# The queries' normed rows are turned by VectorE and placed by DMA instead of being turned by TensorE, and the order of products is rewritten

## The chip, the core and the metric

The kernel runs on one core of one Trainium2 chip, all in fp32. Its metric is the device time of one execution in microseconds (us). Engines are named as in the profile: PE is TensorE's matmul, PEld its weight load, DVE VectorE, ACT ScalarE, POOL GpSimd, SP SyncE. SP and POOL issue nearly all DMAs. Each engine runs its own program in order; a semaphore wait holds everything behind it on that engine.

## The reference

```python
x = x + xattn(layernorm(x), ctx, ctx, Wq, Wk, Wv, Wo)   # 8 batches of 512 rows of 256, ctx 1601 rows
x = x + ffn(layernorm(x), ...)                          # shared FFN and 16 experts, top 64 rows each

def xattn(query, key, value, Wq, Wk, Wv, Wo):           # 16 heads of 16
    q = (query @ Wq.T) * scale; k = key @ Wk.T; v = value @ Wv.T
    scores = sigmoid(q k^T)                             # per head, no softmax
    return (scores @ v) @ Wo.T
```

## The kernel before

**Stages.** The attention of batches b = 0 to 7 runs first; the FFN follows. In each batch's attention there are 52 "quads": 4 quarters of 13 tiles of 128 context rows. A quad is two pairs, each of them S (2 matmuls, L1751, scores of two heads into one of three PSUM banks `score0..2`) and an ACT sigmoid (L876) from the bank to SBUF, and then one W (8 matmul records, L1780, probabilities times values, into `acc` or `misc`).

**Products.** Beside batch b's quads PE makes what batch b + 1 needs: K (keys, L1566), V (values, L1580), Q (queries, L1589), T (the normed rows of x turned, so that rows stand along the free axis, L1597), and what is left of batch b - 1: O (output projection, L1607) and G (gate logits, L1649, into `misc`). All but G go into the same ring of three score banks: whatever stands three ring entries later (S or product) may start only when the entry before it in that bank has been read, by ACT for an S, by DVE for a product (`wait_slot`).

**Order.** The strings OPENING (batch 0), EACH (1 to 6) and CLOSING (7) give PE's order: a letter S or W, or T for "the next product" of the list that `beside(b)` returns. ACT and DVE take up the work in that order. DVE has further work that is keyed to quads (`beside_quad(b, q)`, called at the odd S of quad q): for the residual rows of batch b - 1 the sums at q 9, the scale at 11, `norm_apply` and `turn_norm` (32x32 block transposes into `norm_blocks`) at 12 and `split_norm` at 22; for the x rows of batch b + 1 sums at 15, scale at 17, apply at 19 (17, 19, 21 in batch 0).

**Placing.** DVE's transposes turn 32x32 blocks only. `place_norm` on POOL moves the blocks with 16 DMAs of 32 KB (L765); it waits until SP's two stores of the batch (`norm_scr`, `resid_scr`, semaphore `post_stored`) have landed. `split_norm` waits for all 16 (`norm_placed`) and makes a high and a low part (`nt_hi`, `nt_lo`), which SP stores at q 24. After that store (`nt_stored`) the T products of x fill the same two tiles, `turned_rows` reading them from PSUM, and Q reads them.

**Tiles.** `xn` holds x and then its normed rows; `resid` holds x again (loaded by SP at q 24) to take the O products of the next batch.

## Time and profile before

| what | us |
|---|---|
| median of 3 runs | 1311.09 (1307.8 to 1319.05) |
| the profiled run, its time | 1305.85 |
| the profiled execution, its span | 1304.0 |
| the attention part, to the start of the FFN | about 892 |
| one batch, 1 to 6 | 109.0 |
| PE busy / ACT busy in such a batch | 108.3 / 98.8 |

The clock that TensorE was granted is 1.00 of full speed in every window. PE is busy in all but 0.7 us of a batch by the profile's count, ACT nine tenths of it, DVE 54%, POOL a tenth. A busy PE is not a PE without waits, since the records of matmuls in flight overlap; the starts of its instructions tell more than its busy share.

### The profile page before, as it was taken

What the parts mean: (1) busy time and instruction counts of PE and PEld (TensorE: products, weight loads), DVE (VectorE), ACT (ScalarE), POOL (GpSimd) and SP (SyncE); (2) the same over time, 40 slices, a digit from 0 to 9 for tenths busy, and PEclk for the clock granted to TensorE, in tenths of its full rate; (3) what the DMA queues carried; (4) which work ended last, traced back from release to release, by engine and by line L of the source; (5) the groups of instructions that cost most, each with busy time, mean ns of one, the idle gap of its engine ahead of it and who ended that gap; (6) DMA issues with size and microseconds to landing.
All of it is one profiled execution on the core that took longest, in us unless ns stands there. A gap on an engine that the chain in (4) does not pass through costs nothing.

```text
span 1304.0 us, 25503 instructions
## 1 busy us (share of the span) xinstructions
PE 1283.8 (98%) x10200; PEld 772.1 (59%) x10200; DVE 732.5 (56%) x1377; ACT 985.3 (76%) x1148; POOL 286.9 (22%) x288
## 2 busy tenths in 40 slices
PE   8999999999999999999999999999999999999997
PEld 6445444444454544544444443336888888888887
DVE  6564475365266448437536633215558777777773
ACT  5888989998998899899999989996333455555553
POOL 3000030020002003002000200500001567677635
PEclk9999999999999999999999999999999999999999
DMA  7785973874776597387477549713543577777754
GB/s 215 179 188 126 139 184 111 125 162 133 130 139 166 118 137 171 113 131 148 149 129 140 127 93 156 169 34 114 195 130 110 181 201 192 188 192 190 192 109 49
DMA packets 118726, 190.82 MB, mean 146 GB/s; under 512 B 22448, under 2 KB 71600, under 8 KB 118608
## 3 DMA queue, kind: packets, MB, share of 16 engines
q1 hardware_dynamic: 98768, 155.21, 51.9%
q0 software_dynamic: 19648, 33.72, 12.4%
q8 instruction: 81, 1.33, 0.5%
q10 hardware_dynamic: 192, 0.26, 0.1%
q14 instruction: 37, 0.30, 0.1%
HBM read 108.43 MB, written 55.61 MB: 126 GB/s over the span
## 4 chain that ended last, share of the span: by engine, by line
PE 87%; issue 5%; DMA 2%; DVE 2%; ACT 2%; POOL 1%; SPq 0%; POOLq 0%; DVEq 0%; ACTq 0%
PE score L1839 19%; PE score L1751 18%; PE acc L1780 14%; PE misc L1780 13%; PE score L1857 9%; PE score L1566 5%; PE score L1580 5%; PE score L1589 2%; ACT probs L876 1%; PE score L1619 1%; PE score L1607 1%; DMA key_scr<-key_parts 1%; POOL norm L765 1%; DMA norm<-norm_blocks 1%; DMA ctx_raw<-ctx_t 1%
## 5 line engine op out<-in xcount | busy, mean ns | idle before, releaser
L876 ACT ACTIVATE probs<-score 128x1024 f32<-128x1024 f32 (+1 forms) x832 | 789.8, 1026 | 77.3 <-PE score L1751 70.6
L1751 PE MATMUL score<-queries,keys 48*128 48x512 f32 (+1 forms) x1664 | 312.2, 438 | 6.5 <-ACT probs L876 4.2
L1751 PEld LDWEIGHTS score<-queries,keys 48*128 48x128 f32 (+1 forms) x1664 | 139.1, 180 | 275.0 <-ACT probs L876 212.7
L1780 PE MATMUL acc<-probs,values 128*32 128x512 f32 (+1 forms) x1664 | 210.5, 601 | 0.0
L1780 PE MATMUL misc<-probs,values 128*32 128x512 f32 (+1 forms) x1664 | 205.8, 600 | 0.0
L1026 DVE TENSOR_REDUCE whole<-score 128x512 f32<-128x1024 f32 (+1 forms) x75 | 77.0, 1026 | 196.6 <-PE score L1566 119.6
L729 POOL DMA_DIRECT2D ctx_raw<-ctx_t x32 | 23.4, 733 | 642.6 <-DVE ctx_lo L1004 557.9
L801 POOL DMA_INDIRECT gathered<-norm_scr,gather_row x64 | 81.2, 1269 | 227.5 <-DVE gather_row L1374 212.2
L891 ACT ACTIVATE gelu<-score 128x512 f32<-128x512 f32 (+1 forms) x97 | 55.5, 580 | 84.6 <-PE score L1839 84.0
L814 POOL DMA_INDIRECT out<-result,add_row x64 | 106.6, 1666 | 48.4 <-ACT result L944 25.9
L1839 PE MATMUL score<-tok_hi,gu_hi 128*128 128x512 f32 (+1 forms) x388 | 117.0, 383 | 0.0
L1839 PE MATMUL score<-tok_lo,gu_hi 128*128 128x512 f32 (+1 forms) x388 | 116.2, 381 | 0.0
L1839 PE MATMUL score<-tok_hi,gu_lo 128*128 128x512 f32 (+1 forms) x388 | 116.2, 381 | 0.0
L1321 DVE TENSOR_TENSOR hidden<-gelu,score 128x512 f32<-128x512 f32 (+1 forms) x97 | 64.0, 664 | 92.6 <-PE score L1839 62.3
L899 ACT ACTIVATE hid_hi<-hidden 128x512 fp32r<-128x512 f32 (+1 forms) x100 | 61.0, 613 | 63.9 <-DVE hidden L1321 60.7
L1066 DVE TENSOR_REDUCE values<-score 128x512 f32<-128x1024 f32 (+1 forms) x52 | 59.3, 1141 | 71.7 <-PE score L1580 71.0
L1780 PEld LDWEIGHTS misc<-probs,values 128*32 128x32 f32 (+1 forms) x1664 | 40.7, 108 | 87.0 <-issue 76.6
L1780 PEld LDWEIGHTS acc<-probs,values 128*32 128x32 f32 (+1 forms) x1664 | 38.8, 108 | 77.0 <-issue 71.5
L1839 PEld LDWEIGHTS score<-tok_lo,gu_hi 128*128 128x128 f32 x388 | 71.8, 188 | 14.2
L1839 PEld LDWEIGHTS score<-tok_hi,gu_lo 128*128 128x128 f32 x388 | 71.8, 188 | 14.1
L1839 PEld LDWEIGHTS score<-tok_hi,gu_hi 128*128 128x128 f32 x388 | 70.2, 189 | 12.9 <-issue 0.8
L944 ACT ACTIVATE result<-score,add_w 128x256 f32<-128x256 f32 x60 | 23.6, 474 | 67.9 <-DVE add_w L1364 64.7
(257 smaller groups left out, 1626.2 us busy)
## 6 DMA issues: line engine op xcount, KB each, us to landing
keys<-key_scr SPq DMA_DIRECT2D x180, 200.2 KB, 8.0
key_scr<-key_parts SPq DMA_DIRECT2D x45, 512.0 KB, 8.3
gu_raw<-w_gu SPq DMA_DIRECT2D x17, 1024.0 KB
ctx_raw<-ctx_t POOLq DMA_DIRECT2D x24, 512.0 KB, 5.1
queries<-query_parts SPq DMA_DIRECT2D x186, 64.0 KB, 2.5
d_raw<-w_d SPq DMA_DIRECT2D x17, 512.0 KB
norm<-xn SPq DMA_DIRECT2D x224, 32.0 KB
xn<-x SPq DMA_DIRECT2D x8, 512.0 KB, 3.8
```

The costliest lines, as they stand in the source:

```text
L801: pool.indirect_dma_start(gathered[par][:, t, :], None, norm_scr[:, :], bass.IndirectOffsetOnAxis(ap=gather_row[par][:, t:t + 1], axis=0)) ...
L814: pool.indirect_dma_start(out[:, :], bass.IndirectOffsetOnAxis(ap=add_row[par][:, t:t + 1], axis=0), result[par][:, t, :], None, compute_o ...
L876: act.activation(probs[0:rows, (n + 1) % RING, 2 * pair:2 * pair + 2, :], score[SLOT[k]][0:rows, :, :], ACT.Sigmoid, scale=SCALE).then_inc ...
L899: act.activation(hid_hi[par][:, of, cols], hidden[:, f % 2, cols], ACT.Copy).then_inc(hid_hi_done, 1)
L1026: dve.tensor_reduce(whole[:, 0:n], score[SLOT[task]][:, :, 0:n].rearrange("p e s -> p s e"), AX_X, ALU.add).then_inc(halves_added, 1)
L1321: dve.tensor_tensor(hidden[:, f % 2, cols], gelu[:, f % 2, cols], of, ALU.mult).then_inc(hidden_done, 1)
L1566: mm = pe.matmul(bank[:, e, 0:n], W2[a][rows, WK, k, P * half:P * (half + 1)], parts_of_ctx(b, kc)[c][rows, k, 0:n], start=(j == 0 and k = ...
L1580: mm = pe.matmul(bank[0:n, e, D * i:D * (i + 1)], parts_of_ctx(b, kc)[a][rows, k, s0:s0 + n], W2[c][rows, WV, k, :], start=(j == 0 and k = ...
L1751: mm = pe.matmul(score[SLOT[k]][0:rows, g, :], keys[quarter % KEY_RING][of, pair, P * st:P * st + rows], queries[half][of, e, pair, :], st ...
L1780: mm = pe.matmul(sums_bank[n // NST % 2][32 * c:32 * (c + 1), :], values[b % 2][0:rows, st, half, c, :], probs[0:rows, (n + 1) % RING, c, ...
L1839: mm = pe.matmul(bank[:, f % 2, cols], (gu_hi, gu_lo)[a][slot][:, w, k, P * of:P * (of + 1)], (tok_hi, tok_lo)[b][par][:, k, cols], start= ...
L1857: mm = pe.matmul(d_bank[:, t2, D * (t % 2):D * (t % 2 + 1)], (hid_hi, hid_lo)[a][par][:, f, P * t:P * (t + 1)], (d_hi, d_lo)[b][slot][:, f ...
```

## The change

The two T products of batches 1 to 7 are gone from PE and from the ring. In their place:

- DVE turns the normed x rows in 32x32 blocks from `xn` into the tile of `resid` (`turn_x`, at quad 20, in batch 0 at 22).
- POOL places the blocks back into `xn` with 16 DMAs (`place_x`), after `place_norm`. The loads of the next context chunks are issued behind it.
- DVE makes the two parts from SBUF (`split_x`, at quad 28, in batch 0 at 32). PE's Q waits for it.
- `resid` is reloaded after the blocks have left it, at the Q product, instead of at quad 24; the next x load also stands there and waits for `x_split`.
- Both T's leave the list, K(c,1,2) and V(c,2,0) move ahead of Q(c,0), and the order strings are new.

```diff
--- before.py
+++ after.py
@@ -110,27 +110,26 @@
     if c < B:
         out += [("V", c, 0, 0), ("V", c, 0, 1),
                 ("K", c, 0, 1), ("K", c, 1, 1), ("V", c, 1, 0), ("V", c, 1, 1),
-                ("T", c, 0), ("T", c, 1), ("Q", c, 0), ("K", c, 0, 2)]
+                ("K", c, 0, 2), ("K", c, 1, 2), ("V", c, 2, 0), ("Q", c, 0)]
     else:
         out += UPS[:2]
     if b:
         out += [("G", b - 1)]
     if c < B:
-        out += [("K", c, 1, 2), ("V", c, 2, 0), ("V", c, 2, 1),
-                ("K", c, 0, 3), ("K", c, 1, 3), ("V", c, 3, 0), ("Q", c, 1)]
+        out += [("V", c, 2, 1), ("K", c, 0, 3), ("K", c, 1, 3), ("V", c, 3, 0), ("Q", c, 1)]
     else:
         out += UPS[2:]
...
-EACH = ("SSWWSSTSWSSSWWSTSTSSWWSSTSSWSSSWWSSTSSWSSSWWSSTSWSSSWWSTSTSSWWSSSWWSSSWWSSTSWSSTSWSSSWWSTS"
-        "WSSSWWSSSWWSTSWSSTSWSSTSWSSSWTWSSTSWSSTSWSSTSWSSSWWSTTSSWSTSWSSSWWSSSWWSSTSWSSSWWSSSWWSS")
...
+EACH = ("SWWSSSWWSSTSWSSTSWSSTSWSSTSTSSWWSSTSWSSSWWSSSWWSSTSWSSSWWSSSWWSSTSWSSSWWSSSWWSSTSWSSTSWSSS"
+        "WWSSSWWSSTSWSSTSWSSSWWSSTSTSSWTSSSWWSSSWWSSTSWSSSWWSTTSSWSSWSTSWSSTSWSSSWWSSSWWSSSWWSS")
...
@@ -359,6 +358,9 @@
         last_out = logits[:].rearrange("p t b e -> p (t b e)")[:, 0:P]
         choice = logits_t
+        x_raw = xn[:].rearrange("p t d -> p (t d)").rearrange("p (k s) -> p k s", s=S)
+        x_blocks = resid[:].rearrange("p t d -> p (t d)").rearrange("p (j c) -> p j c", c=P)
+
         score = [keep.enter_context(nc.psum_tensor(f"score{i}", [P, 2, S], F32)) for i in range(3)]
         acc = keep.enter_context(nc.psum_tensor("acc", [P, S], F32))
         misc = keep.enter_context(nc.psum_tensor("misc", [P, S], F32))
@@ -528,15 +533,17 @@
                 engine.wait_ge(queries_in[half], STACK_DMAS * (2 * b + 1 + half))
             def load_resid_a(b):
-                if b:
+                if b + 1 < B:
+                    sp.wait_ge(x_placed, PLACE_DMAS * (b + 1))
+                else:
                     sp.wait_ge(post_stored, STORE * b)
+                sp.dma_start(resid[:], x_rows[b]).then_inc(x_again_in, 16)
+
+            def load_x(b):
+                if b > 1:
+                    sp.wait_ge(x_split, b - 1)
                 else:
-                    sp.wait_ge(direct_written, 16 * len(DIRECT))
-                    sp.wait_ge(first_keys_in[2], STACK_DMAS)
-                sp.dma_start(resid[:], x_rows[b]).then_inc(x_again_in, 16)
-
-            def load_x(b):
-                sp.wait_ge(misc_copied, COUNT["T", b - 1, KC - 1])
+                    sp.wait_ge(misc_copied, COUNT["T", 0, KC - 1])
                 sp.dma_start(xn[:], x_rows[b]).then_inc(x_in, 16)
             def store_norm(b):
@@ -602,8 +609,6 @@
                 write_keys(("K", 0, 0, kc))
             for b in range(B):
                 for what, which in STEPS[b]:
-                    if what == "S" and which == 2 * QPB // 2:
-                        load_resid_a(0)
                     if what == "S" and b:
                         q = which % (2 * QPB) / 2
                         if q == 0:
@@ -623,7 +628,8 @@
                             stack_keys(4 * b + 3)
                         if q == 24:
                             store_norm_t(b - 1)
-                            load_resid_a(b)
+                            if b + 1 == B:
+                                load_resid_a(b)
                     if what == "T":
                         task = which
                         if task[:3] == ("K", 0, 0):
@@ -643,8 +649,10 @@
                         elif task[0] == "Q":
                             if task[1] == 0 or task[2] == 0:
                                 stack_queries(*task[1:])
-                        elif task[0] == "T" and task[2] == KC - 1 and task[1] + 1 < B:
-                            load_x(task[1] + 1)
+                            if task[1] and task[2] == 0:
+                                load_resid_a(task[1] - 1)
+                                if task[1] + 1 < B:
+                                    load_x(task[1] + 1)
                         elif task == ("G", b - 1):
                             place_gates(b - 1)
@@ -765,11 +773,24 @@
                         pool.dma_start(tok_raw[TURN * j:TURN * (j + 1), :, P * i:P * (i + 1)],
                                        norm_blocks[TURN * i:TURN * (i + 1), j::BLOCKS, :]).then_inc(norm_placed, 16)
+            def place_x(b):
+
+                pool.wait_ge(x_turned, b)
+                for i in range(BLOCKS):
+                    for j in range(BLOCKS):
+                        pool.dma_start(x_raw[TURN * j:TURN * (j + 1), :, P * i:P * (i + 1)],
+                                       x_blocks[TURN * i:TURN * (i + 1), j::BLOCKS, :]).then_inc(x_placed, 16)
+
+            for kc in range(NCH - 1):
+                load_ctx(1, kc)
             for b in range(1, B):
-                for kc in range(NCH):
-                    load_ctx(b, kc)
+                load_ctx(b, NCH - 1)
                 if b >= 2:
                     place_norm(b - 2)
+                place_x(b)
+                if b + 1 < B:
+                    for kc in range(NCH - 1):
+                        load_ctx(b + 1, kc)
             def split_lo(which, slot, s):
@@ -1158,20 +1179,27 @@
                 dve.wait_ge(split_step, s.now())
                 dve.tensor_tensor(two, bank[:, 1, :], two, ALU.add).then_inc(misc_copied, 1)
-            def turned_rows(task):
-
-                k, by_half = task[2], "p (t e c) -> p e t c"
-                dve.wait_ge(misc_full, COUNT[task])
-                rows = score[SLOT[task]][:, :, 0:TT * ROWS].rearrange("p e (t c) -> p e t c", c=ROWS)
-                hi = nt_hi[:, k, :].rearrange(by_half, t=TT, e=2)
-                lo = nt_lo[:, k, :].rearrange(by_half, t=TT, e=2)
-                for e in range(2):
-                    last = dve.tensor_copy(hi[:, e], rows[:, e])
-                last.then_inc(split_step, s.up())
-                dve.wait_ge(split_step, s.now())
-                for e in range(2):
-                    last = dve.tensor_tensor(lo[:, e], rows[:, e], hi[:, e].bitcast(F32), ALU.subtract)
-                last.then_inc(misc_copied, 1)
+            def turn_x(b):
+                dve.wait_ge(xn_ready, b + 1)
+                if b == 1:
+                    dve.wait_ge(direct_written, 16 * len(DIRECT))
+                    dve.wait_ge(first_keys_in[2], STACK_DMAS)
+                else:
+                    dve.wait_ge(post_stored, STORE * (b - 1))
+                dve.transpose(x_blocks.rearrange("p j (t q) -> p t j q", q=TURN),
+                              xn[:].rearrange("p t (j q) -> p t j q", q=TURN)).then_inc(x_turned, 1)
+
+            def split_x(b):
+                wait_past(dve, nt_stored, STORE * (b - 1))
+                dve.wait_ge(x_placed, PLACE_DMAS * b)
+                for k in range(KC):
+                    raw = x_raw[:, k, :].rearrange("p (i t q) -> p t i q", i=BLOCKS, q=TURN)
+                    hi = nt_hi[:, k, :].rearrange("p (t i q) -> p t i q", i=BLOCKS, q=TURN)
+                    lo = nt_lo[:, k, :].rearrange("p (t i q) -> p t i q", i=BLOCKS, q=TURN)
+                    dve.tensor_copy(hi, raw).then_inc(split_step, s.up())
+                    dve.wait_ge(split_step, s.now())
+                    last = dve.tensor_tensor(lo, raw, hi.bitcast(F32), ALU.subtract)
+                last.then_inc(x_split, 1)
             def early_ups(task):
@@ -1223,12 +1251,7 @@
                     early_ups(task)
                 else:
                     k = task[2]
-                    if kind == "T" and k == 0:
-                        wait_past(dve, nt_stored, STORE * (b - 1))
-                    if kind == "T" and task not in FIRST:
-                        turned_rows(task)
-                    else:
-                        two_parts(task, nt_hi[:, k, :], nt_lo[:, k, :])
+                    two_parts(task, nt_hi[:, k, :], nt_lo[:, k, :])
                 if kind in "KV" and LAST_OF[b, task[3] if kind == "K" else task[2]] == task:
                     kc = task[3] if kind == "K" else task[2]
                     if (b, kc) == (0, 0) or (b and kc == 1):
@@ -1291,6 +1314,10 @@
                     norm_scale()
                 if b + 1 < B and q == (21 if b == 0 else 19):
                     norm_apply(xn, xn, xn_ready)
+                if b + 1 < B and q == (22 if b == 0 else 20):
+                    turn_x(b + 1)
+                if b + 1 < B and q == (32 if b == 0 else 28):
+                    split_x(b + 1)
             for b in range(B):
                 for what, which in STEPS[b]:
@@ -1591,13 +1618,6 @@
                                            start=(j == 0 and k == 0), stop=(j == 2 and k == KC - 1))
                 return mm
-            def turned_halves(tile, k, bank):
-                for t in range(TT):
-                    for e, rows in enumerate(ROW_TILES):
-                        mm = pe.transpose(bank[:, e, ROWS * t:ROWS * (t + 1)], tile[rows, t, P * k:P * (k + 1)],
-                                          ident[rows, rows])
-                return mm
-
             def out_halves(b, t2, bank):
                 pe.wait_ge(o_split, 2 * (b + 1))
                 for t in range(2 * t2, 2 * t2 + 2):
@@ -1705,12 +1725,11 @@
                 elif kind == "V":
                     mm = value_product(task, bank)
                 elif kind == "Q":
+                    if b:
+                        pe.wait_ge(x_split, b)
                     mm = query_halves(task[2], bank)
                 elif kind == "U":
                     mm = up_halves(task, bank)
-                elif kind == "T":
-                    pe.wait_ge(xn_ready, b + 1)
-                    mm = turned_halves(xn, task[2], bank)
                 elif kind == "O" and b + 1 < B:
                     if b == 0 and task[2] == 0:
                         pe.wait_ge(w_split, 3)
```

The first place is DVE from the products O to the turned norm rows, in a batch of the middle. Before:

```order
L1157 TENSOR_TENSOR resid<-score,resid 128x512
L1159 TENSOR_TENSOR resid<-score,resid 128x512
L1157 TENSOR_TENSOR resid<-score,resid 128x512
L1159 TENSOR_TENSOR resid<-score,resid 128x512
L1087 BN_STATS bn<-resid 128x6 x4
L1066 TENSOR_REDUCE values<-score 128x512
```

The bn_aggr, scale, norm and transpose instructions follow here. Now:

```order
L1178 TENSOR_TENSOR resid<-score,resid 128x512
L1180 TENSOR_TENSOR resid<-score,resid 128x512
L1178 TENSOR_TENSOR resid<-score,resid 128x512
L1180 TENSOR_TENSOR resid<-score,resid 128x512
L1087 TENSOR_REDUCE values<-score 128x512
L1108 BN_STATS bn<-resid 128x6 x4
L1087 TENSOR_REDUCE values<-score 128x512
L1023 CAST ctx_hi<-ctx_raw 128x1024
L1025 TENSOR_TENSOR ctx_lo<-ctx_raw,ctx_hi 128x1024
```

Two V reductions and the two parts of a context chunk (L1023, L1025) now stand ahead of the norm's scale; before, one V reduction did.

The second place is DVE from the normed x rows to the parts, quads 19 to 28. Before (a V reduction stands ahead of the parts of the norm, L1200 and L1202):

```order
L1117 TENSOR_SCALAR xn<-xn,mv,rs 128x256 x4
L1066 TENSOR_REDUCE values<-score 128x512
L1200 CAST nt_hi<-norm 128x512
L1202 TENSOR_TENSOR nt_lo<-norm,nt_hi 128x512
L1200 CAST nt_hi<-norm 128x512
L1202 TENSOR_TENSOR nt_lo<-norm,nt_hi 128x512
L1066 TENSOR_REDUCE values<-score 128x512
L1002 CAST ctx_hi<-ctx_raw 128x1024
L1004 TENSOR_TENSOR ctx_lo<-ctx_raw,ctx_hi 128x1024
L1002 CAST ctx_tail<-ctx_raw 128x132
L1004 TENSOR_TENSOR ctx_tail<-ctx_raw,ctx_tail 128x132
```

Now:

```order
L1138 TENSOR_SCALAR xn<-xn,mv,rs 128x256 x4
L1189 STREAM_TRANSPOSE resid<-xn 128x4x8x32
L1228 CAST nt_hi<-norm 128x512
L1230 TENSOR_TENSOR nt_lo<-norm,nt_hi 128x512
L1228 CAST nt_hi<-norm 128x512
L1230 TENSOR_TENSOR nt_lo<-norm,nt_hi 128x512
L1087 TENSOR_REDUCE values<-score 128x512 x2
L1023 CAST ctx_hi<-ctx_raw 128x1024
L1025 TENSOR_TENSOR ctx_lo<-ctx_raw,ctx_hi 128x1024
L1023 CAST ctx_tail<-ctx_raw 128x132
L1025 TENSOR_TENSOR ctx_tail<-ctx_raw,ctx_tail 128x132
L1156 SCALAR_TENSOR_TENSOR o_sum<-misc,mine,o_sum 128x512
```

The transpose of xn is new, and the parts of the norm (L1228, L1230) stand ahead of both V reductions.

The third place is PE around the first T product (L1597). Before:

```order
L1751 MATMUL score<-queries,keys 65x512 x2
L1780 MATMUL misc<-probs,values 32x512 x8
L1751 MATMUL score<-queries,keys 65x512 x2
L1597 MATMUL score<-ident,xn 128x64 x8
L1751 MATMUL score<-queries,keys 128x512 x2
L1780 MATMUL misc<-probs,values 32x512 x4
```

Now, in the same stretch of the program, where the short last tile (65 rows) marks the same quad:

```order
L1770 MATMUL score<-queries,keys 65x512 x2
L1799 MATMUL misc<-probs,values 32x512 x4
L1770 MATMUL score<-queries,keys 65x512 x2
L1770 MATMUL score<-queries,keys 128x512 x4
L1799 MATMUL misc<-probs,values 32x512 x8
L1770 MATMUL score<-queries,keys 128x512 x6
```

The 8 transposing matmuls between two S are gone.

## Rows read from the trace of the kernel before

**Rows 1.** The page: busy time by engine.
```profile
PE 1283.8 (98%) x10200; PEld 772.1 (59%) x10200; DVE 732.5 (56%) x1377; ACT 985.3 (76%) x1148; POOL 286.9 (22%) x288
```

**Rows 2.** Windows: length, busy PE, PEld, DVE, ACT, POOL (instructions), clock, DMA share, GB/s.
```profile
573.00:682.00 109.00, 108.28 (x984) 50.76 (x980) 58.77 (x119) 98.87 (x105) 11.41 (x20) 1.00 0.67 141
```

**Rows 3.** Waits of the span: who for whom, us, times, longest us.
```profile
PEld score L1751 <- ACT probs L876: 212.7, 296, 0.8
ACT probs L876 <- PE score L1751: 70.6, 160, 1.3
```

**Rows 4.** Timeline of PE, the S ahead and the W behind of both T's: start, us.
```profile
628.81 0.45 PE L1751 MATMUL score<-queries,keys 48*65 48x512 f32 x2
...
630.02 1.06 PE L1780 MATMUL misc<-probs,values 128*32 128x512 f32 x8
...
636.76 0.50 PE L1751 MATMUL score<-queries,keys 48*128 48x512 f32 x2
...
637.72 1.06 PE L1780 MATMUL acc<-probs,values 128*32 128x512 f32 x8
```

**Rows 5.** The chain in order of time: start, us, what (8 records are a W).
```profile
604.29 0.99 PE acc L1780 x8
605.29 0.90 PE score L1751 x6
606.18 1.86 PE acc L1780 x16
...
608.47 1.39 PE score L1566 x12
```

**Rows 6.** Timeline of DVE, 597 to 608: from V to the turned norm.
```profile
597.41 1.23 DVE L1066 TENSOR_REDUCE values<-score 128x512 f32<-128x1024 f32 x1 [4.03 <-PE score L1580]
598.55 0.37 DVE L1092 BATCH_NORM_AGGREGATE mv<-bn 128x2 f32<-128x6 f32 x4
...
602.75 1.25 DVE L1191 STREAM_TRANSPOSE norm_blocks<-norm 128x1024 f32<-128x1024 f32 x1
...
605.25 0.68 DVE L1002 CAST ctx_hi<-ctx_raw 128x1024 fp32r<-128x1024 f32 x1
...
607.11 1.40 DVE L1087 BATCH_NORM_STATS2 bn<-xn 128x6 f32<-128x256 f32 x4
```

**Rows 7.** Timeline of SP, then the landing time of all L546 issues.
```profile
603.15 0.51 SPq L546 DMA_DIRECT2D resid_scr<-resid  x1
...
DMA to landing us min/median/max: 4.4/4.4/7.2
```

**Rows 8.** Timeline of POOL, then landings of the issues 608 to 617.
```profile
608.21 8.51 POOL L765 DMA_DIRECT2D norm<-norm_blocks  x16
...
DMA to landing us min/median/max: 6.0/8.0/10.1
```

**Rows 9.** Timeline of DVE, 611 to 634.
```profile
612.49 1.23 DVE L1026 TENSOR_REDUCE whole<-score 128x512 f32<-128x1024 f32 x1
...
618.00 1.38 DVE L1117 TENSOR_SCALAR xn<-xn,mv,rs 128x256 f32<-128x256 f32 x4
...
622.80 0.42 DVE L1200 CAST nt_hi<-norm 128x512 fp32r<-128x512 f32 x1
...
624.94 1.22 DVE L1066 TENSOR_REDUCE values<-score 128x512 f32<-128x1024 f32 x1
...
633.91 0.75 DVE L1135 SCALAR_TENSOR_TENSOR o_sum<-misc,mine,o_sum 128x512 f32<-128x512 f32 x1 [2.74 <-PE misc L1780]
```

**Rows 10.** The placing that was slowest and the one that was quickest.
```profile
280.55 8.51 POOL L765 DMA_DIRECT2D norm<-norm_blocks  x16
...
295.82 0.43 DVE L1200 CAST nt_hi<-norm 128x512 fp32r<-128x512 f32 x1 [0.58 <-DMA norm<-norm_blocks]
...
827.29 1.61 POOL L765 DMA_DIRECT2D norm<-norm_blocks  x3
...
837.66 0.43 DVE L1200 CAST nt_hi<-norm 128x512 fp32r<-128x512 f32 x1 [15.15 <-DMA norm<-norm_blocks]
```

## What the change should do to the time, worked out before it ran

> **What bounds the kernel now.** I read the page's busy times first. PE is busy 98% of the span, ACT 76%, DVE 56%, POOL 22% [rows 1]. The change touches only the attention part, so the second view is the windows: in one batch of 109.0 us PE is busy 108.3, ACT 98.9, DVE 58.8 and POOL 11.4, at a full clock [rows 2]. So a batch's length is PE's list of work plus what PE waits. The waits of the span say how: PE's weight loads wait for ACT to empty a score bank 296 times, never more than 0.8 us, and ACT waits for scores 160 times, 70.6 us in all [rows 3]. PE and ACT run close, and ACT has some 10 us of slack in a batch: what is taken from PE shortens a batch, and each us for which PE stands still lengthens it. DVE is far from full, but it works in order and its reading of a product frees a score bank: a late DVE can stop PE. There I look for the danger.
>
> **What is taken from PE.** With a T, a batch has S T S W at two places. From the S ahead of T to the W behind took 630.02 - 628.81 = 1.21 us and 637.72 - 636.76 = 0.96 us [rows 4]. Without it S S W is left, two S at 0.30 (six records are three S, 0.90 us) [rows 5], so 0.60 each. Saved: 0.61 + 0.36 = 0.97 us a batch, in seven batches 6.8 us. Other gains of the new order (pairs of W instead of single ones: 1.86 against 2 x 0.99 [rows 5], so 0.1 us for each) I leave out. DVE's share stays: four reads of a T go, a transpose (1.25 [rows 6]) and two pairs of parts (2.14, as for the norm: 624.94 - 622.80 [rows 9]) come.
>
> **What the new order does to the norm.** The work for the norm of batch b - 1 starts later on DVE, and its parts now stand ahead of a V that PE has just made. I count in us from the moment when PE ends V(c,0,1), the product ahead of DVE's norm work.
>
> DVE: V is read, 598.55 - 597.41 = 1.14; the two parts of the context chunk that now stand ahead, 607.11 - 605.25 = 1.86; scale and apply, 602.75 - 598.55 = 4.20 [rows 6]. The norm is ready at 7.2. SP issues the store of resid 0.4 later and it lands 4.4 after that [rows 6, 7], at 12.0, and with it POOL may begin `place_norm` at 12.1. The 16 issues take 8.5 us, and the last, issued at 8.0, lands at least 6.0 later [rows 8]: 14.0, and 0.3 until DVE starts. I take 14.3. The bounds are the slowest placing, 295.82 - 280.55 = 15.3, and the quickest, 837.66 - 827.29 = 10.4 [rows 10]. The parts of the norm can start at 26.4.
>
> DVE is there much earlier. K(c,1,1) ends on PE at 17.6 (in the new EACH 18 S at 0.30, two single W at 0.99, four pairs at 1.86, two K at 1.39 [rows 5]: 5.4 + 2.0 + 7.4 + 2.8). Its reading and parts take 1.23 + 1.07 = 2.3 (1.07 is half of the 2.14 above), xn is applied in 1.4 [rows 9] and turned in 1.25 [rows 6]: 22.5. DVE then stands for 3.9 us at `norm_placed`, and behind it in its queue is V(c,1,0).
>
> PE ends V(c,1,0) at 26.4 (27 S, six pairs and three single W, K, K, V at the price of K: 8.1 + 11.2 + 3.0 + 4.2). The S that takes V's bank is the third ring entry behind it, after S, W, S: 0.30 + 0.99 + 0.30 = 1.6, at 28.0. DVE starts the parts at 26.4, needs 2.14, then reads V in 1.23 [rows 9]: 29.8. **PE stands for 1.8 us** in each of batches 1 to 6, 10.8 us. With a placing of 15.3 it is 2.8 us, with 10.4 nothing. Before, the V at that place (quad 21.5) was read before the parts of the norm, and they began at 622.80 with no wait [rows 9]. Where the stall goes: PE is the engine with no slack, ACT's bank runs dry meanwhile, and dense products follow, so I take all of it as lost.
>
> A rule of the Trainium skill would make the stall vanish. "DMA: Bandwidth & Descriptors", section "Anatomy of one DMA — SWDGE (gpsimd) path", gives a DMA from GpSimd's queue about 2.0 us and its bytes at 436 GB/s, so 2.1 us for 32 KB, an estimate from that page. By it the last issue at 8.0 would land at 10.1, DVE would find the norm in place at 22.5, and the time would be that of rival B. The trace shows 6.0 to 10.1 us for each of these [rows 8].
>
> **What place_x costs.** POOL is free of the norm at 12.1 + 8.5 = 20.6 and xn is turned at 22.5, so it issues from 22.6 to 31.1 and x is placed at 36.9. POOL has 98 of 109 us free [rows 2]; the next context load stands behind it, where DVE frees its buffer only at about 31. `split_x` stands on DVE behind the sums of quarter 1, whose last W ends on PE at 26.4 + 9.2 = 35.6 (ten S, V, five W), with the stall 37.4. The sums take 0.75 [rows 9] and a pair of parts, 1.8: 39.2. So x is there with 2.3 us to spare and DVE does not wait; its parts end at 41.3. K(c,0,2) ended on PE at 38.5 + 1.8 = 40.3; it is read at 42.5, while its bank is wanted at 41.9. **Another 0.6 us** a batch, 3.6 us in six. Bounds: nothing, and 1.6. PE's own wait for `x_split` at Q, five quads later, costs nothing. The moved reload of resid has until the next batch's O, and its DMA count is the same. The 3.7 MB more between SBUF tiles I cost at nothing, the DMA engines being busy 0.67 [rows 2].
>
> **Batch 0** has no norm: only the saving. **Batch 7** has no T and keeps its time. One thing more is left at nothing: from the last Q to the first K of the next batch the order now has nine quads without a product, before 6.5. There PE can wait for ACT more, or less since more W's stand there; the longest such wait is 0.8 us [rows 3], so this is worth -0.8 to +0.8 a batch, 5 us either way.
>
> **The sum.** -6.8 + 10.8 + 3.6 = +7.6 us. Against the profiled execution's span of 1304.0 (its time 1305.85) that is 1311.6. The median of the runs before is 1311.1, 5 us above the profiled run; against it the forecast is 1318.7.
>
> **The rivals.**
>
> A, the forecast: 1318.7, chance 0.55.
>
> B, the norm is in time. For it: the quickest placing took 10.4, and DVE reaches the parts at 22.5, just when the norm would be there; a gain that I left out would push the same way. Against it: that placing ran in batch 7, where few other transfers run, and those in the middle took 14 and more [rows 8, 10]. Then -6.8 + 3.6 = -3.2, 1307.9. It decides below a placing of about 12.6 (1.8 less than 14.3). This is the side of a gain. Chance 0.27.
>
> C, slower by more: POOL's queue is the bound. The x blocks are issued 22.6 us in, before the norm's have landed, into the same queue. If both are slow, 15.3 for the norm and 3 us more for x, V's stall is 2.8 and x is placed at 40.9, while DVE is there at 40.2: 0.7 more on K. Six times 1.0 + 0.7 is 10.2 more: 1329. It decides from x later than 39.2 in the count of the forecast. For it: DVE has 2.3 us to spare, no more; against it: POOL is idle between and the 16 engines aren't full. Chance 0.18.
>
> That the change does nothing (a T costs PE nothing) is not a case: the rows show 0.97 us.
>
> **Numbers.** About 1% (13 us) is what a measurement of this kernel can tell from no change: below 1298 is faster, above 1324.2 slower. B and nearly all of its spread lie within; A reaches 1324.2 with +5.5, which the nine quads or a placing 0.9 us slower would bring, so a fifth of it and most of C are slower: 0.28. Faster needs B and the 5 us of the nine quads and more, 0.05; same 0.67. The range takes in B with its spread and C: 1303 to 1332. For A alone it is 1312 to 1326.
>
> **What would show it.** Right: in the trace after, DVE idles 3 to 5 us ahead of the first part of the norm, released by the DMA norm<-norm_blocks, in six batches; PE's weight loads for scores wait for DVE values about 2 us there; `split_x` waits for nothing; a batch lasts 109.0 - 1.0 + 2.4 = 110.4 us. Wrong: if DVE waits less than 2 us at the norm, B holds and a batch lasts some 108.6; if DVE waits for xn<-resid, C. If a batch lasts under 107.5, the order gives more than I counted. The price of one sigmoid and the FFN part should not move.

## The result and the profile after

The changed kernel takes 1324.21 us, median of five executions (1323.5 to 1335.93), against 1311.09 (1307.8 to 1319.05), a median of five too. The ratio is 1.0133, 95% interval 1.0103 to 1.0164: slower, by 13 to 22 us. The profiled execution has a span of 1322.4 us against 1304.0, and a mean granted clock of 0.994.

The page's first line answers [rows 1]. PE is as busy as before, with 112 instructions less; POOL has 112 DMAs more to issue:

```profile
PE 1289.4 (98%) x10088; PEld 767.3 (58%) x10088; DVE 734.3 (56%) x1356; ACT 985.6 (75%) x1148; POOL 349.4 (26%) x400
```

The length of a batch is read from the start of its first S to that of the next one's. Before, batch 0 took 111.7 us and batches 1 to 6 took 109.0 to 109.1, but for batch 2 with 109.5. After, they are, from batch 0 on, 113.3, 111.3, 112.5, 112.6, 112.8, 110.3 and 110.5. Two of them as windows (columns as in [rows 2]), batch 5 and batch 3:

```profile
587.50:697.80 110.30, 108.47 (x964) 49.76 (x965) 58.80 (x116) 99.20 (x105) 20.01 (x36) 1.00 0.69 142
362.20:474.80 112.60, 110.02 (x966) 50.94 (x966) 58.88 (x116) 99.10 (x105) 20.06 (x36) 0.98 0.67 140
```

Batch 5 is what the forecast gave (110.4). Batch 3 has the same instructions and is 2.3 us longer, at a mean clock of 0.98. The waits of the span (us in all, times, longest) answer [rows 3]:

```profile
PEld score L1770 <- ACT probs L897: 208.5, 288, 0.8
ACT probs L897 <- PE score L1770: 86.2, 182, 2.0
POOL norm L773 <- DMA resid_scr<-resid: 50.1, 6, 8.6
DVE nt_hi L1228 <- DMA norm<-norm_blocks: 36.8, 7, 15.6
POOL xn L781 <- DVE resid L1189: 17.5, 7, 3.5
PEld score L1770 <- DVE values L1087: 11.0, 7, 2.2
PE score L1770 <- DVE values L1087: 8.2, 6, 1.9
```

DVE waits for the placing of the norm in all seven batches that have one, 15.6 us in batch 7 and about 3.5 in each of the six others. The last two rows are PE waiting for DVE to read `values`. Before, such a wait was never longer than 0.8 us (9 of them, 7.1 us in all, by the same view), and now they reach 2.2. Batch 3 in the timelines. POOL (start, us; in brackets the idle time ahead), whose first row answers [rows 8]:

```profile
398.39 8.66 POOL L773 DMA_DIRECT2D norm<-norm_blocks  x16 [8.29 <-DMA resid_scr<-resid]
409.48 7.96 POOL L781 DMA_DIRECT2D xn<-resid  x15 [2.43 <-DVE resid L1189]
```

DVE, which answers [rows 9]:

```profile
407.94 1.25 DVE L1189 STREAM_TRANSPOSE resid<-xn 128x1024 f32<-128x1024 f32 x1
412.92 0.54 DVE L1228 CAST nt_hi<-norm 128x512 fp32r<-128x512 f32 x1 [3.73 <-DMA norm<-norm_blocks]
...
414.56 0.69 DVE L1230 TENSOR_TENSOR nt_lo<-norm,nt_hi 128x512 fp32r<-128x512 f32 x1
415.16 1.22 DVE L1087 TENSOR_REDUCE values<-score 128x512 f32<-128x1024 f32 x1
```

PE:

```profile
414.30 0.51 PE L1770 MATMUL score<-queries,keys 48*128 48x512 f32 x2
416.44 0.60 PE L1770 MATMUL score<-queries,keys 48*128 48x512 f32 x2 [1.63 <-DVE values L1087]
416.83 0.63 PE L1607 MATMUL score<-w_hi,ctx_hi 64*128 64x256 f32 x4
...
419.39 0.63 PE L1770 MATMUL score<-queries,keys 48*65 48x512 f32 x2
```

DVE has turned x at 409.2 and stands for 3.73 us until the last block of the norm is there, 14.5 us after POOL's first issue. Only then come the parts and the reading of V(c,1,0), at 415.16. PE's two S at 414.30 and 416.44 start 2.14 us apart where such a pair otherwise starts 0.34 apart: 1.8 us lost. In batches 1 to 6 that distance is 1.60, 2.15, 2.13, 2.37, 1.44 and 1.55 us, so the loss is 9.2 us in all.

What follows was not forecast. The product behind the stall, V(c,1,1), took 419.39 - 416.83 = 2.56 us; it takes 1.39 at the full clock (batch 5). The windows of 2 us show why (the number behind the last bracket is the clock):

```profile
415.00:417.00 2.00, 0.56 (x4) 0.47 (x6) 1.38 (x2) 0.87 (x1) 2.00 (x5) 0.93 0.60 214
417.00:419.00 2.00, 2.00 (x24) 2.00 (x22) 0.00 (x0) 1.02 (x1) 0.45 (x1) 0.50 1.01 360
419.00:421.00 2.00, 2.00 (x18) 0.61 (x16) 1.37 (x2) 0.94 (x1) 0.54 (x1) 0.72 0.25 67
421.00:423.00 2.00, 2.00 (x22) 0.84 (x22) 1.93 (x4) 1.60 (x3) 0.00 (x0) 1.00 0.00 0
```

PE was granted 0.50, its lower level (1.2 GHz), from the end of the stall on, for 3.4 us in all. This stands behind the three longest stalls (batches 2, 3 and 4), not behind the three shorter ones, and costs about 1.45 us each time.

The second stall that was forecast is behind K(c,0,2), DVE first and then PE:

```profile
429.32 0.69 DVE L1201 TENSOR_TENSOR nt_lo<-xn,nt_hi 128x512 fp32r<-128x512 f32 x1
429.93 1.22 DVE L1047 TENSOR_REDUCE whole<-score 128x512 f32<-128x1024 f32 x1
```

```profile
429.96 0.50 PE L1770 MATMUL score<-queries,keys 48*128 48x512 f32 x2
431.20 0.50 PE L1770 MATMUL score<-queries,keys 48*128 48x512 f32 x2 [0.74 <-DVE whole L1047]
```

K is read behind `split_x`, and the next S starts 1.24 us behind its neighbour instead of 0.34. In the six batches the distance is 1.14 to 1.24, so 0.8 to 0.9 us lost in each, 5 us in all.

The third loss occurs once, at the start of batch 1. SP's queue, then PE:

```profile
111.36 7.56 SPq L527 DMA_DIRECT2D queries<-query_parts  x12
118.96 0.58 SPq L540 DMA_DIRECT2D resid<-x  x1
119.59 1.59 SPq L547 DMA_DIRECT2D xn<-x  x1
121.23 1.02 SPq L496 DMA_DIRECT2D key_scr<-key_parts  x2
126.23 7.54 SPq L510 DMA_DIRECT2D keys<-key_scr  x12
```

```profile
138.34 0.49 PE L1770 MATMUL score<-queries,keys 48*128 48x512 f32 x2 [2.97 <-DMA keys<-key_scr]
```

The moved loads of `resid` and `xn` (0.5 MB each) stand on SP ahead of the writes of the keys, and PE waits 2.97 us for the keys of batch 1 (the writes are L496, the loads of keys L510). Before, the 12 loads of keys began at 122.11, and PE did not wait for them.

From the start of batch 7 to the end it is 514.1 against 512.8 us.

One thing more stands in this trace. The 16 blocks of x are issued right behind those of the norm and are as large, but in batch 3 they land 1.7 to 3.9 us after their issue, and the norm's 6.3 to 10.1. The stretches of the two sets of issues as windows (the last number but one is the busy share of the 16 DMA engines):

```profile
398.40:406.50 8.10, 8.10 (x66) 3.28 (x62) 5.72 (x22) 7.57 (x9) 8.10 (x15) 1.00 1.00 120
409.50:419.10 9.60, 7.97 (x80) 5.07 (x74) 3.40 (x5) 6.86 (x8) 7.95 (x15) 0.88 0.78 232
```

The norm is placed while the DMA engines are full, x when they are not. The other batches show the same (see the last section).

### The profile page after: what moved, and what is told of

It reads as the page before. It is cut to its first block and busy times, and to the rows that moved or that the text cites. A ratio compares the mean times of both kernels' runs of the same rounds, so it can differ in the third digit from the quotient of the medians.

```text
span 1322.4 us, 25376 instructions
## 1 busy us (share of the span) xinstructions
PE 1289.4 (98%) x10088; PEld 767.3 (58%) x10088; DVE 734.3 (56%) x1356; ACT 985.6 (75%) x1148; POOL 349.4 (26%) x400
## 3 DMA queue, kind: packets, MB, share of 16 engines
q0 software_dynamic: 23232, 37.40, 12.8%
## 5 line engine op out<-in xcount | busy, mean ns | idle before, releaser
L1799 PE MATMUL misc<-probs,values 128*32 128x512 f32 (+1 forms) x1664 | 208.5, 601 | 0.0
L835 POOL DMA_INDIRECT out<-result,add_row x64 | 108.3, 1692 | 46.8 <-ACT result L965 24.3
L1858 PEld LDWEIGHTS score<-tok_lo,gu_hi 128*128 128x128 f32 x388 | 71.8, 188 | 14.3
L1858 PEld LDWEIGHTS score<-tok_hi,gu_hi 128*128 128x128 f32 x388 | 69.8, 189 | 15.6 <-issue 3.4
```

The costliest lines, as they stand in the source:

```text
L835: pool.indirect_dma_start(out[:, :], bass.IndirectOffsetOnAxis(ap=add_row[par][:, t:t + 1], axis=0), result[par][:, t, :], None, compute_o ...
L1799: mm = pe.matmul(sums_bank[n // NST % 2][32 * c:32 * (c + 1), :], values[b % 2][0:rows, st, half, c, :], probs[0:rows, (n + 1) % RING, c, ...
L1858: mm = pe.matmul(bank[:, f % 2, cols], (gu_hi, gu_lo)[a][slot][:, w, k, P * of:P * (of + 1)], (tok_hi, tok_lo)[b][par][:, k, cols], start= ...
```

## The experiments

My theory (N): the placing of the norm lands late in the new order, and DVE, standing for it, holds up V(c,1,0). The rivals: PE's bank is held for another reason (P: DVE's load or the traffic of x), or the loss is in the new order itself (O). Beside the first four experiments the kernel before took 1309.09 us (median of ten executions, 1306.41 to 1320.4), beside the last four 1307.16 (19 executions).

### The parts of the norm two quads later

```diff
-                if b and q == 22:
+                if b and q == 24:
                     split_norm(b - 1)
```

> Edit: in the changed kernel the parts of the norm are made at quad 24 instead of 22, so that V(c,1,0) is read ahead of them. Theory N (the order of DVE's work and the norm that lands late make PE stand, and TensorE's clock falls to half behind the longer stalls): the 1.1 to 2.0 us by which the S at quad 24 is late in six batches goes, and with it the three stretches of 3.4 us at half clock. 6 x 1.8 + 3 x 1.5 = 15 us: near 1309, a batch near 110 us, clock 1.0 throughout. Rival P (the 16 more DMAs of x in POOL's queue slow everything behind them): the wait only moves to the next product, 1320 or more. Rival O (the new order of products costs time by itself, whatever DVE does): no more than 5 us go, 1319 or more.

Measured: 1315.49 us (1310.24 to 1320.63), ratio 1.0065 [1.0041, 1.0090]; the profiled execution 1308.4. Batch 3 as a window, and DVE there:

```profile
359.70:468.70 109.00, 108.14 (x964) 49.66 (x965) 58.73 (x116) 98.95 (x105) 20.16 (x36) 1.00 0.69 144
```

```profile
410.59 1.23 DVE L1087 TENSOR_REDUCE values<-score 128x512 f32<-128x1024 f32 x1 [3.98 <-PE score L1607]
411.73 0.42 DVE L1228 CAST nt_hi<-norm 128x512 fp32r<-128x512 f32 x1
```

V is read first, as soon as PE has made it, and behind it the norm is there: the wait of DVE is gone from batches 1 to 6, the two S stand 0.34 us apart in all six, and no half clock follows. Batches 2 to 6 take 109.0 to 109.1 us. The placing itself is as long as in the kernel after (14.3 and 14.5 us from the first issue to the last landing in batch 3), and only the place of the parts in DVE's order was changed: what makes the stall is that DVE stands for the late norm ahead of V(c,1,0). The stall behind K (1.06 to 1.18 us) and the wait for the keys of batch 1 (4.16 us, here followed by a stretch at half clock that costs 1.7 us more) remain. The time did not fall as far as expected, 1309: by the ratios the edit gives 0.7%, about 9 us of the 15. The profiled execution shows 14 (1322.4 to 1308.4), but it is the fastest of five that spread over 10 us, at mean clocks of 0.996 down to 0.993, so the other four had more time at half clock than the trace has.

### The parts of x at quad 32 in every batch

```diff
-                if b + 1 < B and q == (32 if b == 0 else 28):
+                if b + 1 < B and q == 32:
                     split_x(b + 1)
```

> Edit: in the changed kernel the parts of x are made at quad 32 in every batch instead of at 28, behind the reads of K(c,0,2) and K(c,1,2). Theory N: the 0.8 to 0.9 us by which the S behind K(c,0,2) is late in six batches goes, 5 us: near 1319; the stall at quad 24 and the falls of the clock stay. Rival P: nothing changes or PE's Q waits for the parts, 1324 or more.

Measured: 1320.42 us (1320.19 to 1323.99), ratio 1.0104 [1.0081, 1.0127]. The distance at K is 0.34 us in every batch; the stall at V stays (1.38 to 2.72 us in batches 1 to 6). That is 0.3% less than the kernel after, about 4 us, for the 5 us that the rows promise, and near the 1319 that was expected.

### The two loads behind the keys

```diff
-                            if task[1] and task[2] == 0:
-                                load_resid_a(task[1] - 1)
-                                if task[1] + 1 < B:
-                                    load_x(task[1] + 1)
...
                             stack_keys(4 * b + 5)
+                            load_resid_a(b)
+                            if b + 2 < B:
+                                load_x(b + 2)
```

> Edit: in the changed kernel the reload of resid and the next load of x stand on SP behind the loads of the next batch's keys instead of between the queries' copies and the key writes. Theory: at the start of batch 1 PE waits 3.0 us for keys; the two loads hold SP for 2.2 us ahead of the last key writes, so the wait falls to about 1 us and the time by 2 us, to 1322; nothing else changes, since in the other batches keys are in time. Rival (the wait at that place has to do with the moved products Q and K of batch 0 alone): the wait stays at 3 us.

Measured: 1318.61 us (1316.66 to 1321.83), ratio 1.0088 [1.0063, 1.0113]. SP's queue and PE:

```profile
118.71 1.18 SPq L496 DMA_DIRECT2D key_scr<-key_parts  x2
123.32 7.55 SPq L510 DMA_DIRECT2D keys<-key_scr  x12
130.91 0.58 SPq L540 DMA_DIRECT2D resid<-x  x1
```

```profile
135.58 0.50 PE L1769 MATMUL score<-queries,keys 48*128 48x512 f32 x2 [0.42 <-DMA keys<-key_scr]
```

The keys are fetched 2.9 us earlier and PE waits 0.42 us instead of 2.97; about 1 us was expected. Batch 0 takes 110.6 us. The gain, 0.45% or about 6 us, is larger than the 3 us of the profiled execution of after; in its second profile, and in three other kernels that had the loads ahead of the keys, this wait was 4.2 to 4.8 us, each time with a stretch at half clock behind it.

### All three

The three edits above together.

> Edit: the three edits together (parts of the norm at quad 24, parts of x at 32, the two loads behind the keys). If the three places are all that the change costs, and the T products save 6 to 7 us: 1311 - 6.8 + 1 = near 1305, a batch near 108.2 us. If a cost is left that I have not seen, it is above 1309. Rival O: above 1315.

Measured: 1301.82 us (1300.42 to 1302.07), ratio 0.9951 [0.9932, 0.9969]. It beats both kernels, and the expected 1305 by 3 us. Batch 3:

```profile
352.50:460.70 108.20, 107.98 (x965) 49.74 (x966) 58.74 (x116) 98.77 (x105) 20.16 (x36) 1.00 0.70 144
```

Batch 0 takes 110.2 us and batches 1 to 6 take 108.9, 108.2, 108.2, 108.7, 108.2 and 108.3: the change as it was made, without its three delays. It gives 24 us back against the kernel after, and none of its executions is slower than 1302.07. DVE turns and splits x and POOL issues its 16 DMAs as in the kernel after, and PE's only two waits in batches 1 to 6 are for ACT, 1.0 us in all: once the steps are at these places, no stall of PE comes of that path.

### The kernel before without the T's

This kernel and the next leave the turning of x out for batches 1 to 7.

```diff
-                ("T", c, 0), ("T", c, 1), ("Q", c, 0), ("K", c, 0, 2)]
+                ("Q", c, 0), ("K", c, 0, 2)]
```

(and the two letters T taken from each of OPENING and EACH. What waited for a T waits for something else: the load of the next x stands at Q and waits for the normed rows, and Q waits for the parts of the norm. All else is in its place.)

> The kernel before with the T products taken out of its order and nothing put in their place: the order is otherwise that of before, Q takes the parts that lie in SBUF (those of the previous norm), and the turning of x for batches 1 to 7 is left out, so the output is not the reference's. It measures the price of the T's alone. My sum said 0.97 us a batch in seven batches, -6.8 us: a batch of 109.1 becomes 108.1 to 108.3, and the time is 6 to 7 us under that of the kernel before (ratio 0.995). In the kernel after with its three delays removed a batch took 108.2, which fits that. Rival: the T's sat in PE time that ACT needed anyway, and a batch stays within 0.3 us of 109.1. The clock stays at 1.00, and DVE does not wait for norm<-norm_blocks in batches 1 to 6.

Measured: 1302.71 us (median of ten, 1302.19 to 1313.54), ratio 0.9966 [0.9940, 0.9993], or 4.4 us. An undisturbed batch (batch 5):

```profile
572.80:681.40 108.60, 107.65 (x966) 49.85 (x965) 55.75 (x111) 98.73 (x105) 11.41 (x20) 1.00 0.67 140
```

Batches 1, 3, 5 and 6 take 108.5 to 108.6 against 109.0 to 109.1: the two T's cost about 0.5 us a batch, neither the 0.97 that I had counted nor the 0.3 or less of the rival. Batches 2 and 4 take 109.6 and 108.9. There DVE waited 1.02 and 0.39 us for the norm, which was not expected, and the two S behind V's bank stand 1.25 and 0.64 us apart. The starts of PE show where the rest went: at each of the two places one S now stands 0.57 and 0.53 us ahead of the next element, where 0.23 to 0.34 is usual. PE waits for its bank there, which ACT empties, and a T had filled part of that time.

### The kernel after without x's path

```diff
-                place_x(b)
...
-                if b + 1 < B and q == (22 if b == 0 else 20):
-                    turn_x(b + 1)
-                if b + 1 < B and q == (32 if b == 0 else 28):
-                    split_x(b + 1)
```

(Here too the waits that named a step of x's path name another: the reload of `resid` waits for the stores of the norm, the load of x for the normed rows, Q for the parts of the norm.)

> The kernel after, order and place of the norm's parts (quad 22) as in it, without turn_x, place_x and split_x: Q takes the parts of the previous norm, so the turning of x for batches 1 to 7 is left out and the output is not the reference's. It tells whether the stall ahead of V(c,1,0) is the norm's own lateness or made by the new traffic. Theory N (the norm is late because DVE's work for it begins late in the new order): the wait of DVE for norm<-norm_blocks stays at 3 to 5 us in each of six batches, a little longer than in the kernel after since DVE has no turn_x ahead of it, PE still stands 1.0 to 1.8 us there, and the stall behind K(c,0,2) is gone; a batch lasts 109.8 to 111, the time is 2 to 6 us over the kernel before. Rival P (the transfers of x hold the norm up, or the 1.25 us of turn_x hold up V): the placing takes 12 us or less and PE's stall there vanishes; a batch of 108.3, the time 5 us under the kernel before.

Measured: 1317.5 us (1314.4 to 1322.89), ratio 1.0063 [1.0033, 1.0092]. Its waits:

```profile
DVE nt_hi L1228 <- DMA norm<-norm_blocks: 47.7, 7, 18.2
PEld score L1766 <- DVE values L1087: 11.5, 7, 2.4
```

With 1.25 us less of work for DVE ahead of it, and no block of x moved, DVE waits longer for the norm (4.9 us a batch without batch 7's, against 3.5), and PE's stall is the same: distances of 2.37, 2.22, 1.49, 2.54, 1.88 and 1.25 us. The distance at K is 0.34. So the traffic of x is not what delays the norm, and rival P is out. PE waits 4.77 us for the keys of batch 1 here too: it is the two loads, not the blocks of x. The time is about 8 us over the kernel before by the ratio, where 2 to 6 were expected: I had left out that wait and the three stretches at half clock (one behind it, two behind V's stalls of batches 2 and 4).

### Stalls of rising length in the kernel before

```diff
                 if b and q == 22:
+                    dve.wait_ge(norm_placed, PLACE_DMAS * b)
+                    for i in range(b if b < B - 1 else 0):
+                        dve.wait_ge(split_step, s.now())
+                        dve.tensor_tensor(...ALU.add).then_inc(split_step, s.up())   # 128x512, idle work
                     split_norm(b - 1)
```

> The kernel before, its work unchanged, with idle work on DVE ahead of the parts of the norm at quad 22: b additions of 0.7 us in batch b for b = 1 to 6, none in batch 7. It makes stalls of PE of rising length at one place, to see which of them the granted clock follows. DVE has nothing late there in the kernel before, so batch 1 and 2 should show a stall of PE under 0.8 us and keep the full clock; from batch 3 on the stall behind V(c,1,0) or behind a T grows by about 0.7 us a batch to some 3 us in batch 6. Theory: stalls of PE of 2 us and more are followed by a stretch at half clock of about 3.4 us that costs some 1.5 us on top; so batch 5 and 6 at least show it, and 1 to 3 do not. Rival: the half clock in the kernel after came of something else of that order, and no stall here is followed by it.

Measured, one execution: 1334.93 us, a span of 1333.1. The distance of the two S behind the held bank was 0.70, 2.21, 2.17, 2.93, 3.64 and 4.34 us in batches 1 to 6. From batch 3 on it grows by 0.7 us with each addition, as expected; batch 2, where I had expected less than 0.8, has 2.21. DVE shows why:

```profile
296.38 0.69 DVE L1290 TENSOR_TENSOR norm_blocks<-w_hi,w_lo 128x512 f32<-128x512 f32 x1 [0.66 <-DMA norm<-norm_blocks]
```

In batch 2 DVE has to wait 0.66 us for the norm before the first of the additions. It did so in the kernel before too (0.58 us, the slowest placing of [rows 10]), and the two S stood 0.79 us apart there. That and two additions of 0.7 us are 2.2. The expectation that DVE has nothing late at that place did not hold for batch 2.

The half clock followed in batches 2, 4, 5 and 6, not in 1 and 3. PE in batch 5 and the windows around it:

```profile
638.36 1.22 PE L1758 MATMUL score<-queries,keys 48*128 48x512 f32 x4 [3.13 <-DVE values L1066]
639.52 3.64 PE L1787 MATMUL misc<-probs,values 128*32 128x512 f32 x16
```

```profile
640.00:644.00 4.00, 4.00 (x28) 1.13 (x20) 0.61 (x3) 1.31 (x3) 1.45 (x2) 0.50 0.98 292
644.00:658.00 14.00, 14.00 (x116) 6.05 (x116) 7.24 (x14) 13.03 (x14) 0.00 (x0) 1.00 0.28 86
```

Two W took 3.64 us (1.92 at the full clock). Without its stall a batch took 108.9 us where no half clock came (1, 3), 110.3 where it lasted 3.4 us (2, 4), and 111.5 where it lasted 6.7 us (5, 6). In its own profile the kernel before has no such stretch ahead of its last 3 us, and only additions on DVE were put in, so a stall of PE can bring it: one of 3.3 us on PE costs 5.9. It does not take a long one. At the start of batch 7 of this run 3.4 us at half clock follow two idle times of 0.51 and 0.41 us, which the kernel before has there too, at the full clock.

### The kernel after once more

The same kernel, run beside the last three.

> The kernel after, unchanged, on the chip and in the call of the kernels without T and without x's path. 1.010 to 1.015 of the kernel before. Its profile shows whether the lengths of the stalls and the stretches at half clock stand in the same batches: stalls of 1.4 to 2.4 us behind V(c,1,0) in batches 1 to 6 as before; if the half clock follows the longer ones again it is tied to the stall, but the batches need not be 2, 3 and 4.

Measured: 1322.68 us (1322.37 to 1325.89), ratio 1.0115 [1.0070, 1.0161]. The distances at V were 2.84, 2.22, 1.70, 2.44, 1.66 and 1.59 us, and only the second was followed by the half clock. The longest was not: PE, and its window:

```profile
196.03 0.50 PE L1770 MATMUL score<-queries,keys 48*128 48x512 f32 x2 [2.34 <-DVE values L1087]
196.37 0.40 PE L1607 MATMUL score<-w_hi,ctx_hi 64*128 64x256 f32 x4
```

```profile
195.00:199.00 4.00, 2.97 (x36) 1.89 (x36) 1.99 (x2) 1.80 (x2) 2.02 (x4) 1.00 0.88 307
```

So "the longer stalls bring the half clock" holds only in part. Over the six profiles in which such a stall was seen (36 batches; this kernel stands among them twice), it followed none of the distances up to 2.13 us but one (the 2.13 of batch 3 above), 9 of the 16 between 2.15 and 2.93 us, and both above. The length alone does not decide, and what else does is left open here.

## Why the prediction was right, and where it wasn't

The time forecast was 1318.7 (1303 to 1332), the measured one is 1324.2: inside, at the very bound that the prediction had set between no change and slower. Rival A was the case, and its two stalls came at the places and by the waits that it names. The size of the change was too small: +7.6 us was forecast, and +13.1 came between the medians, +18.4 between the spans. That the time lies only 5.5 us off is in part luck, since the median of before lay 5 us above the profiled execution and that of after on it. The terms, from one profiled execution to the other (1311.6 forecast, 1322.4 found):

| term | forecast | measured |
|---|---|---|
| T's gone and new order, batches 0 to 6 | -6.8 | -5.8 |
| V(c,1,0) held by the wait for the norm | +10.8 | +9.2 |
| K(c,0,2) behind `split_x` | +3.6 | +5 |
| half clock behind the stalls | not seen | +4.4 |
| keys of batch 1 behind the moved loads | 0 | +3.0 |
| from batch 7 to the end | 0 | +1.3 |

These add up to 17.1 of the 18.4 us; the rest is in pieces of 0.3 us and less.

**The saving.** The size was nearly right for the wrong reason. The T's alone are worth 0.5 us a batch (the kernel without them), because the two places then run into ACT. "Without it S S W is left, two S at 0.30" was the step that failed: [rows 4] were priced as if ACT had a bank free. The new order, which I had left out, is what is left for the other 0.3 to 0.4 (108.2 with all three repairs against 108.6); no run changes it alone. The measured term in the table is that kernel against the kernel before: -1.5 in batch 0 and -4.3 in the six others.

**The norm.** Each link stood in the trace: placing 14.3 forecast, 14.5 found; DVE's wait 3.9 forecast, 3.73 in batch 3; PE's stall 1.8 forecast, 1.1 to 2.0 found. Moving the parts by two quads removed PE's stall, and taking x's path out did not, so the cause is shown. The rule from the Trainium skill that was weighed ("DMA: Bandwidth & Descriptors", "Anatomy of one DMA — SWDGE (gpsimd) path") would have had the last block in place 2.1 us after its issue, by about 409, and rival B true. DVE was released at 412.92, so the trace does not agree for the norm. For x it nearly does: the last block of batch 3 landed 1.8 us after its issue. So it is not 16 DMAs in a row that make a landing of 6 us and more; it goes with the DMA engines being full in the norm's stretch, which the prediction's landing times from [rows 8] had in them.

**K behind `split_x`.** The mechanism was right, the size 0.6 instead of 0.85. `split_x` waited for nothing, as forecast. Rival C (x late) did not occur: the last issue ended at 419.7 and `split_x` began at 427.80, 8.1 us apart as forecast and without a wait. The placing of x was taken to be as slow as the norm's, 14.3 us. It took 10.6 to 12.8 in batches 1 to 6, so x was there 3.7 to 7.4 us ahead of `split_x`, not 2.3, and C was farther off than the prediction held.

**The clock.** The prediction took a stall of PE at its own length. Three of six cost 1.45 us more, the term "half clock" in the table. This made the difference between a batch of 110.4 and one of 112.6.

**The batch boundary.** The two loads were moved ahead of other steps on SP, and the prediction did not follow that through. They were checked for who needs what they bring ("has until the next batch's O"), not for what stands behind them on SP. In batch 0 those are the writes of the keys.

## What to carry to other kernels

When an edit lets an in-order engine meet a wait earlier, look at what is queued behind the wait and put the waiting step behind the product that it would hold up: here two numbers and two moved loads turned +1.3% into -0.5%. A load that is moved can cost time through what stands behind it in its queue, even if nobody waits for the load. A landing time read in one stretch holds for a stretch where the DMA engines are as full. An op taken from the bound engine gives back less than its length where the next engine is close behind: price it as the difference to the wait that then appears.

## What the runs showed of the hardware

- **A stall of TensorE can cost more than its length.** Behind many of the longer stalls, in a kernel that otherwise keeps PE busy 98% of the time, the granted clock went to 0.50 for 3.4 us, and for 6.7 behind the two longest of the kernel with the additions; that cost some 1.4 and 2.6 us. Length alone does not tell: the wait of 2.97 us for keys in the kernel after was not followed by it, idle times of 0.51 and 0.41 us at the start of batch 7 of the kernel with the additions were. The Trainium skill ("TensorE: Matmul & The Clock Gate", "What's actually happening") says that the clock has two levels and goes by how busy the engine has been; the trace agrees: the granted clock is 1.00 or 0.50, and windows over a change show a blend of the two, as 0.72. Mean clock and time go together from one execution to the next: the kernel before, 19 executions, from 1305.08 us at 0.999 to 1318.39 at 0.993; the kernel after 1323.5 at 0.995 and 1335.93 at 0.987. So the slower executions of the kernel before have time at half clock as well (some 16 us more at 0.993 than at 0.999, an estimate from these shares of 1310 us); what brings it there, no trace here shows. The version with all three repairs stays at 0.998 or 0.999.
- **The landing time of a DMA goes with how full the engines are.** In the kernel after, the last block of 32 KB of the norm landed 5.6 to 7.0 us after its issue in batches 1 to 6, where the DMA share over the 16 issues was 1.00 to 1.02, and 1.8 in batch 7, where it was 0.49. The last block of x landed after 1.7 to 4.8 us in batches 1 to 6 (share 0.66 to 0.78) and after 7.8 in batch 0 (1.07). No run varies the share by itself.
- **VectorE stood behind GpSimd's arithmetic.** In batch 7 of the kernel with the additions, DVE's application of the norm fell beside POOL's splitting of weights. DVE, then POOL:

```profile
840.77 4.75 DVE L1117 TENSOR_SCALAR norm<-resid,mv,rs 128x256 f32<-128x256 f32 x1
```

```profile
840.79 4.58 POOL L779 TENSOR_TENSOR gu_lo<-gu_raw,gu_hi 128x2048 fp32r<-128x2048 f32 x1
```

  One of four such ops took 4.75 us, and the four 10.29, where [rows 9] have 1.38 for all four of x. The one shown ended 0.15 us after POOL's op, which took 4.58 us, as its like did in the kernel before (4.57). PE waited 5.1 us later in this batch, since this norm was placed late. The Trainium skill ("SBUF — State Buffer", "SBUF: two separate sides") describes an exclusive port pair of the two engines that is held for a whole instruction, and the times agree with that; that these two ops met at this pair is argued from them, no run tests it. The kernels before and after do not meet it, as these two pieces of work lie apart there.
